# LSTM on one core: the new cell written to PSUM for ScalarE and again to SBUF, the output gates scaled on GpSimd

## The reference

```
xW = einsum('ntd,dg->ntg', x, Wx) + b
step: a = xW[t] + prev_h @ Wh
      i, f, o = sigmoid of a's first, second, third 512 columns; g = tanh of the fourth
      next_c = f * prev_c + i * g
      next_h = o * tanh(next_c)
out = x + h of every step
```

## Time and profile before

| | |
|---|---|
| median of 3 runs | 1871.62 us (1871.56 to 1872.72) |
| time of the profiled execution | 1872.67 us |
| its span, first to last instruction | 1870.8 us |
| TensorE busy | 1691.8 us, 90% |
| VectorE busy | 1766.2 us, 94% |
| ScalarE busy | 1084.4 us, 58% |
| GpSimd busy | 168.8 us, 9% |
| mean granted TensorE clock | 0.999 |

### The profile page before, as it was taken

One profiled execution on the slowest core, in us unless ns is written; L12 is line 12 of the kernel. 1 busy time (PEld: TensorE's weight loads), 2 busy tenths in 40 slices (PEclk: granted clock), 3 DMA queues, 4 the chain that ended last, 5 costly groups with the idle time before them and its releaser, 6 DMA issues.

```text
span 1870.8 us, 104928 instructions
## 1 busy us (share of the span) xinstructions
PE 1691.8 (90%) x45116; PEld 1064.5 (57%) x45116; DVE 1766.2 (94%) x9739; ACT 1084.4 (58%) x3985; POOL 168.8 (9%) x536
## 2 busy tenths in 40 slices
PE   1899999999999999999999999999999999999997
PEld 0555555555555555555555555555555555555554
DVE  8999999999999999999999999999999999999998
ACT  4555555555555555555655555555655555556554
POOL 0000000000000000000000000000000000000000
PEclk9999999999999999999999999999999999999999
DMA  5000000000000000000000000000000000000000
GB/s 208 15 26 21 21 25 21 21 21 26 21 21 26 21 21 23 24 21 21 26 20 20 26 21 21 21 26 21 21 26 21 21 23 23 21 21 26 18 12 14
DMA packets 39058, 48.96 MB, mean 26 GB/s; under 512 B 4416, under 2 KB 36160, under 8 KB 38592
## 3 DMA queue, kind: packets, MB, share of 16 engines
q1 hardware_dynamic: 37152, 37.77, 6.4%
q10 hardware_dynamic: 1440, 4.49, 0.6%
HBM read 25.46 MB, written 16.78 MB: 23 GB/s over the span
## 4 chain that ended last, share of the span: by engine, by line
DVE 76%; PE 21%; issue 2%; DMA 1%; ACTq 0%; DVEq 0%
DVE turned L500 21%; PE acc L301 12%; DVE mailbox L504 12%; DVE products L513 10%; PE acc L307 8%; DVE o_gate L518 6%; DVE h_halves L529 4%; DVE gates L523 4%; DVE h_halves L538 4%; DVE h_feat L533 3%; DVE x_halves L483 3%; DVE out_ring L565 3%; DVE o_preact L508 3%; DVE x_tops L576 2%; DMA wh<-in_wh 1%
## 5 line engine op out<-in xcount | busy, mean ns | idle before, releaser
L301 PE MATMUL acc<-wh_low,h_halves 128*32 128x256 f16 x16384 | 719.6, 274 | 134.4 <-DVE h_halves L529 132.1
L307 PE MATMUL acc<-wh_high,h_halves 128*32 128x256 f16 x16384 | 724.9, 275 | 0.2
L250 ACT ACTIVATE gates<-mailbox 128x96 f32<-128x96 f32 x1024 | 256.3, 250 | 639.6 <-DVE mailbox L504 639.6
L293 PE MATMUL x_acc<-wx_high,x_halves 128*32 128x512 f16 x8192 | 621.0, 380 | 1.1 <-ACT x_acc L224 1.1
L301 PEld LDWEIGHTS acc<-wh_low,h_halves 128*32 128x32 f16 x16384 | 389.7, 96 | 395.0 <-DVE h_halves L529 381.8
L500 DVE STREAM_TRANSPOSE turned<-acc 128x256 f32<-128x256 f32 x1024 | 458.1, 447 | 58.0 <-PE acc L307 52.1
L307 PEld LDWEIGHTS acc<-wh_high,h_halves 128*32 128x32 f16 x16384 | 343.5, 96 | 132.4 <-DVE h_halves L538 6.8
L293 PE MATMUL x_acc<-wx_low,x_halves 128*32 128x512 f16 x4096 | 399.1, 379 | 0.0
L227 ACT ACTIVATE acc<-x_acc,step_mask 128x512 f32<-128x512 f32 x512 | 328.4, 642 | 3.9 <-PE x_acc L293 3.9
L184 POOL TENSOR_TENSOR o_preact<-turned 128x32 f32<-128x32 f32 x512 | 165.6, 323 | 1696.8 <-DVE turned L500 1696.8
L504 DVE TENSOR_TENSOR mailbox<-turned 128x96 f32<-128x96 f32 x1024 | 269.9, 264 | 17.6
(11 more groups left out here) (66 smaller groups left out, 534.8 us busy)
## 6 DMA issues: line engine op xcount, KB each, us to landing
out<-out_ring SPq DMA_DIRECT2D x128, 128.0 KB, 2.1
x_ring<-in_x SPq DMA_DIRECT2D x120, 128.0 KB, 2.9
wx<-in_wx ACTq DMA_DIRECT2D x4, 512.0 KB, 8.1
wx<-in_wx SPq DMA_DIRECT2D x4, 512.0 KB, 8.1
wh<-in_wh SPq DMA_DIRECT2D x4, 512.0 KB, 16.7
wh<-in_wh ACTq DMA_DIRECT2D x4, 512.0 KB, 17.0
x_ring<-in_x SPq DMA_DIRECT2D x2, 512.0 KB, 16.5
b_rows<-in_b ACTq DMA_DIRECT2D x1, 256.0 KB, 21.2
```

What stands on the lines that cost most here:

```text
L250: act.activation(gates[par][n][:, 1:4, :], preact[n].rearrange("p (g c) b -> p g (c b)", c=2), ACT.Tanh, scale=rescale[chunk % 2]).then_in ...
L293: last = pe.matmul(x_acc[pair % 2][32 * j:32 * j + 32], x_halves[:, pair % (CHUNK // 2), c, half], w[:, c].rearrange("p (n q) g -> p q n g ...
L301: pe.matmul(acc[par][32 * j:32 * j + 32, n, 0:GL], h_halves[1 - par][:, c, 0:2], w_low["wh"][:, c, n * Q + j], start=False, stop=False, sk ...
L307: last = pe.matmul(acc[par][32 * j:32 * j + 32, n, 0:GL], h_halves[1 - par][:, c, 1:3], w_high["wh"][:, c, n * Q + j], start=False, stop=c ...
```

## The change

`preact[1]` moves from `mailbox[0]` to `mailbox[1]`. There is a new PSUM tile, `cell[n]`, in `mailbox[n]`. `new_cell(n)` writes to it instead of to SBUF, and `tanh_of_cell(n)` reads it. A new function `keep_cell(n)` computes the same sum a second time on VectorE into the SBUF tile that the next step reads, with a semaphore `cell_kept`; it stands after `full_h(n)`. `output_gate(n)` leaves VectorE, and GpSimd does the same operation for both groups after its add. VectorE waits for `cell_kept` at the end of a step. In the seventh step of a chunk the wait for `x_sum_ready` stands ahead of `add_three(1)`, since `x_sums` and `preact[1]` now share a PSUM bank.

```diff
-        preact = [mailbox[0][:, 96 * n:96 * (n + 1)].rearrange("p (k b) -> p k b", b=B) for n in range(NG)]
+        preact = [mailbox[n][:, 0:96].rearrange("p (k b) -> p k b", b=B) for n in range(NG)]
+        cell = [mailbox[n][:, 128:128 + 2 * B] for n in range(NG)]
...
                 pool.tensor_tensor(o_preact[0][:], turned[0][:, 6:8, 0, :], turned[0][:, 6:8, 1, :], ALU.add)\
                     .then_inc(o_preact_ready[0], 1)
+                par = t % 2
+                following = (t + 1) // CHUNK % 2
+                if t + 1 < T and (t + 1) % CHUNK == 0 or t == 0:
+                    pool.wait_ge(x_scale_ready, (t + 1) // CHUNK + 1)
+                for n in range(NG):
+                    pool.wait_ge(o_ready, NG * t + n + 1)
+                    pool.tensor_scalar(o_gate[n][:], gates[par][n][:, 4, :], 1.0, scales[following][:, 1:2], ALU.add, ALU.mult)\
+                        .then_inc(h_parts_ready[n], 1)
...
                     act.wait_ge(cell_ready, NG * t + n + 1)
-                    act.activation(cell_tanh[n], gates[1 - par][n][:, 0, :], ACT.Tanh, scale=0.5)\
+                    act.activation(cell_tanh[n], cell[n], ACT.Tanh, scale=0.5)\
                         .then_inc(h_parts_ready[n], 1)
...
-                def output_gate(n):
-                    dve.wait_ge(o_ready, nth[n])
-                    dve.tensor_scalar(o_gate[n][:], gates[par][n][:, 4, :], 1.0, scales[following][:, 1:2], ALU.add, ALU.mult)\
-                        .then_inc(h_parts_ready[n], 1)
-
                 def new_cell(n):
                     dve.wait_ge(products_ready, nth[n])
+                    dve.scalar_tensor_tensor(cell[n], products[n][:, 0, :], 0.5, products[n][:, 1, :],
+                                             ALU.mult, ALU.add).then_inc(cell_ready, 1)
+
+                def keep_cell(n):
                     dve.scalar_tensor_tensor(gates[1 - par][n][:, 0, :], products[n][:, 0, :], 0.5, products[n][:, 1, :],
-                                             ALU.mult, ALU.add).then_inc(cell_ready, 1)
+                                             ALU.mult, ALU.add).then_inc(cell_kept, 1)
...
                 gate_products(0)
+                if at == 6 and chunk + 1 < CHUNKS:
+                    dve.wait_ge(x_sum_ready, chunk + 2)
                 add_three(1)
                 new_cell(0)
-                output_gate(0)
                 add_last(1)
                 gate_products(1)
                 high_of_h(0)
-                if at == 6 and chunk + 1 < CHUNKS:
-                    dve.wait_ge(x_sum_ready, chunk + 2)
                 new_cell(1)
                 full_h(0)
-                output_gate(1)
+                keep_cell(0)
                 low_of_h(0)
                 high_of_h(1)
                 full_h(1)
+                keep_cell(1)
                 low_of_h(1)
+                dve.wait_ge(cell_kept, NG * (t + 1))
```

More of the change, by code:

```diff
@@ L132, in lstm_kernel @@
         cell_ready = sem("cell_ready")
+        cell_kept = sem("cell_kept")
         h_parts_ready = [sem(f"h_parts_ready{n}") for n in range(NG)]
```

## The result

The changed kernel takes 1856.09 us (1855.99 to 1856.47, 4 runs), the kernel before 1871.59 (1871.44 to 1872.72, 4 runs): ratio 0.9917, 95% interval 0.9902 to 0.9932. It is 15.5 us faster. The profiled execution took 1856.47 us, its span is 1854.4.

The account below looks back on a forecast made before the run. The bound was a ring of dependent links closing once per step, with VectorE slightly holding TensorE. Saving 0.03 us x 511 = 15.3 from 1872.67 gave 1857.3, less 1.05 for the median: 1856.3; range 1846 to 1900.

Parts of the forecast that it names:

- VectorE's stretch behind the high part of group 0 holds TensorE: Between group 0's high part and group 1's low part, VectorE delays TensorE's matmuls by 0.02 to 0.05 us a step.
- rival C: TensorE has its own reason for the first 16 matmuls' 0.47 us; gain 0 to 0.015, 1864 to 1872 us; chance 0.16.
- 0.03 us a step: Total gain per step, 511 times, 15.3 us less; from 0.02 (10 us) to 0.05 (26 us).
- The moved wait, taken as 0: Wait for `x_sum_ready`, 31 times, moved ahead of `add_three(1)`: equal within 3 us, taken as 0.
- The gate of group 0 is worth nothing: Moving group 0's output gate saves VectorE some 0.1 us ahead of a wait for ScalarE: nothing for the path.
- The gate of group 1, GpSimd's price: GpSimd's gate of group 1 takes 0.32 us (0.23 to 0.43) and is ready in time for group 1's high part.
- Rival A: GpSimd's gate operation is dear: beyond 0.39 us, each 0.01 costs 5.1 us; at 0.45, 1902 us; chance 0.12.
- The cell in PSUM: VectorE's new cell write to PSUM costs 0 to 0.02 us more; ScalarE's tanh from it takes 0.17.
- The second writes cost nothing: After full h, keep_cell(0) leaves VectorE free at 991.24, when the low part may start; keep_cell(1) fits a 0.22 us wait.
- Rival B: GpSimd's group 1 gate holds keep_cell(0) and the low part on VectorE; 0.06 or 0.13 late, 1902 or 1937 us; chance 0.13.

Follow-up runs that it names:

- The small add: Changed kernel plus an unread GpSimd add of two 32-element SBUF inputs behind its two gates each step; 1903.03 against 1873.48 us for the kernel before, ratio 1.0158.

## Why the prediction was right, step by step

The forecast was 1856.3 us and 15.3 us less; measured were 1856.09 and 15.5 less. Two of its terms were off in size, one down and one up, so that the number agrees to 0.2 us is luck; that it lies within 10 to 26 us is not.

- *VectorE's stretch behind the high part of group 0 holds TensorE.* Right. The high part of group 0 kept its place, and 32 matmuls went from 0.92 to 0.90. Under rival C the first 16 would have kept their 0.47; they took 0.45.
- *0.03 us a step.* Slightly too large for an ordinary step: 3.52 against 3.54 in the two steps shown, and over all steps 0.033 less, of which the moved wait has 2.6 us / 511 = 0.005. So 0.027 or 0.028 a step, some 14 us by the two traces; by the medians 15.5 - 2.6 = 12.9. The low part of group 0 came 0.22 behind full h, where I had 0.21.
- *The moved wait, taken as 0.* Mis-sized. I held it to cost the same at both places, since both stand in front of a link of the ring. It brought 2.6 us in a run of its own. What counts is not whether the path goes through the place, but whether what the instruction needs is there 0.07 us early.
- *The gate of group 0 is worth nothing.* Right by itself (ratio 0.9999); beside the cell in PSUM some 2 us, by the trace of the kernel with group 0 as before.
- *The gate of group 1, GpSimd's price.* I took 0.32; it was 0.34 for group 1 and 0.39 for group 0, where 0.29 is its work and the rest was waiting for VectorE. In time all the same: ready 0.07 ahead of the tanh. It also started earlier than in my working, 2.06 behind the transpose and not 2.10: I had ScalarE's last gate 0.13 to 0.15 behind the tanh of cell 0, and it came 0.07 behind it (981.87, 981.94). Rival A needed over 0.39 for group 1.
- *The cell in PSUM.* VectorE's write took 0.20 against 0.19, within my 0 to 0.02. The tanh took 0.18 to 0.19 where I took 0.17. The high part of group 1 waits for the tanh, as in the working; 4 to 5 us of the gain are this.
- *The second writes cost nothing.* Right, and the experiments showed the price without the cover: at the end of the step the kernel is 65 us slower than before, so 80 us slower than the changed kernel; with the gates in the way it is 43.5 us slower than before.
- *Rival B.* Its mechanism is real, and it missed by very little. The gate of group 1 begins ahead of the second write of group 0, which has two SBUF inputs. I had written that the write would have to *start* later. The runs show that a held operation keeps its start and *ends* 0.04 to 0.05 behind GpSimd's. The gate ends at 982.61 and the second write at 982.65, 0.04 behind it, with the 0.18 that it takes anyway: a hold would begin to show just there. The gate ended 2.40 behind the transpose and not 2.42 as in my working. By what the other runs show, those 0.02 more would have made the write end later; that it was spared is luck. The small add beside the low part shows what a hold can cost: it turned 15.5 us of gain into a loss of 29.6 us.

## What to carry to other kernels

A kernel with one ring of dependent small operations gains what is taken out between a link and the engine that waits for it, and nothing from the same operation elsewhere: one gate brought 6 us, its twin 0. Put extra work where the engine waits for its own last result; there it was free, while at the end of the step it cost 80 us. Before giving GpSimd an operation, look at what VectorE runs beside it with two SBUF inputs, and in both directions: GpSimd's operation may be charged with VectorE's time, and one GpSimd operation of 0.25 us in the wrong place cost more than the whole change brought.

## What the runs showed of the hardware

- GpSimd's scaling of 32 elements took 0.29 us where it started 0.13 behind a VectorE operation with two SBUF inputs, 0.31 to 0.32 at 0.04 to 0.05 behind one and 0.34 at 0.01 behind one, with the same end in the last three.
- For group 0 it took 0.39, beside the second add of three gates and the operations that follow it. In the sixteenth step of a chunk it started 0.07 later and took 0.32, with the same end, 1.64 to 1.65 behind the transposes at 1001.32 and 1004.83. So some 0.1 of the 0.39 is waiting:

```profile
1002.57 0.39 POOL L194 TENSOR_SCALAR o_gate<-gates,scales 128x32 f32<-128x32 f32 x1 [0.40 <-ACT gates L265]
1006.16 0.32 POOL L194 TENSOR_SCALAR o_gate<-gates,scales 128x32 f32<-128x32 f32 x1 [0.48 <-ACT gates L265]
```

- VectorE's low part (two SBUF inputs, 0.19 us) took 0.77 beside a GpSimd add of 256 elements that began just ahead of it and 0.29 beside one of 32, 0.21 beside a scaling that began 0.12 ahead, and 0.22 beside one that began 0.01 behind.
- A second wait in front of one instruction on VectorE cost 0.07 us where the instruction's data had only just come (0.11 instead of 0.04 after it), and nothing where the data was there 0.10 ahead. On GpSimd, a second wait made the gate of group 1 start 0.07 later (1.32 and 1.39 us idle before it in the kernel with that gate alone).
- ScalarE's tanh of 32 elements took 0.187 us on the mean from PSUM to PSUM, 0.199 from SBUF to PSUM and, in the gates, 0.226 from SBUF to SBUF.
